# The layer norm behind a causal attention: centring matrix products removed, chunks in pairs, a copy on ScalarE

## The reference, cut to what matters

```
# block B, per head of 8 features, 16 heads; target is _layernorm(x), also the residual
attn = softmax(scores masked to the causal half)
out  = attn @ v
proj = out @ w_proj + b_proj
y    = proj + target
mu, var = mean(y), var(y)
x    = x + (y - mu) * rsqrt(var + 1e-5) * ln_gamma + ln_beta     # called LN M here
# block C
xn   = (x - mean(x)) / sqrt(var(x) + 1e-5)                       # LN C
x    = x + 0.5 * ffn(xn)
```

## The kernel before

| phase | TensorE | VectorE | ScalarE |
|---|---|---|---|
| 0 | `pe_shares` L1449: spreads the inverse denominators | for c = 3 first `dve_invert` L1459; `dve_divide` L1463 | |
| 1 | `pe_project` L1455 | `dve_add` L1467: bias and residual | |
| 2 | LN M centre | copy | square |
| 3 | LN M variance | reciprocal | root |
| 4 | LN M spread | affine, two instructions | |
| 5 | LN C centre | copy | square |
| 6 | LN C variance | reciprocal | root |
| 7 | LN C spread, c < 2 | norm, c < 2 | |

## Time and profile before

### The profile page before, as it was taken

One profiled execution on the slowest core, in us unless ns is written; L12 is line 12 of the kernel. 1 busy time (PEld: TensorE's weight loads), 2 busy tenths in 40 slices (PEclk: granted clock), 3 DMA queues, 4 the chain that ended last, 5 costly groups with the idle time before them and its releaser, 6 DMA issues. The chain is left out here.

```text
span 1345.5 us, 30396 instructions
## 1 busy us (share of the span) xinstructions
PE 1280.2 (95%) x11965; PEld 469.6 (35%) x12028; DVE 1161.1 (86%) x1536; ACT 1056.3 (79%) x2060; POOL 184.0 (14%) x463
## 2 busy tenths in 40 slices
PE   7887999999999998999899999999999999999998
PEld 4343333332333352555322222222222222223454
DVE  6876899999999276765999999999999999998365
ACT  4656788997999826534599999999999999999742
POOL 9234221211111200111100000000000000000100
PEclk9998999999999999899999999999999999999999
DMA  5252210400000003000422000000000000000000
GB/s 133 53 137 42 51 18 14 66 5 12 4 4 4 8 21 79 1 0 30 130 53 53 4 4 12 4 3 4 13 4 3 3 4 13 4 3 3 12 8 24
DMA packets 38526, 35.12 MB, mean 26 GB/s; under 512 B 16080, under 2 KB 31920, under 8 KB 38384
## 3 DMA queue, kind: packets, MB, share of 16 engines
q1 hardware_dynamic: 38384, 33.17, 10.6%
HBM read 17.03 MB, written 9.70 MB: 20 GB/s over the span
## 5 line engine op out<-in xcount | busy, mean ns | idle before, releaser
L1531 DVE TENSOR_REDUCE m_blockmax<-ps 128x2 f32<-128x1024 f32 (+1 forms) x768 | 879.3, 1206 | 26.7 <-PE ps L1352 12.9
L1504 ACT ACTIVATE m_prob<-ps 128x512 f32<-128x512 f32 (+3 forms) x1664 | 845.5, 576 | 46.5 <-PE ps L1390 33.1
L1352 PE MATMUL ps<-m_k_all,m_q_all 64*128 64x512 bf16 (+2 forms) x1732 | 320.0, 374 | 19.6 <-DVE m_blockmax L1531 16.0
L1390 PE MATMUL ps<-m_q_max,m_k_all 64*128 64x512 bf16 (+3 forms) x1664 | 337.3, 366 | 0.5
L1413 PE MATMUL ps<-m_prob,m_v_op 128*9 128x256 f32 x4096 | 317.0, 381 | 0.1
L1352 PEld LDWEIGHTS ps<-m_k_all,m_q_all 64*128 64x128 bf16 x1732 | 81.7, 92 | 347.8 <-DVE m_blockmax L1531 182.0
L1409 PE MATMUL ps<-m_prob,m_v_op 128*9 128x256 f32 (+3 forms) x2560 | 178.1, 351 | 6.2 <-ACT m_pv L1478 5.4
L1390 PEld LDWEIGHTS ps<-m_q_max,m_k_all 64*128 64x128 bf16 x1664 | 143.6, 94 | 91.8 <-ACT m_prob L1504 45.7
L1555 POOL CAST m_maxparts<-m_negmax 128x8 bf16<-128x8 f32 x64 | 14.1, 221 | 712.6 <-DVE m_negmax L1539 707.2
L1413 PEld LDWEIGHTS ps<-m_prob,m_v_op 128*9 128x9 f32 x4096 | 60.9, 88 | 132.2 <-issue 119.0
L803 ACT ACTIVATE m_prob<-ps 128x512 f32<-128x512 f32 x40 | 23.9, 597 | 67.3 <-PE ps L667 55.5
(11 more groups left out here) (226 smaller groups left out, 1043.5 us busy)
## 6 DMA issues: line engine op xcount, KB each, us to landing
m_part<-m_xn SPq DMA_DIRECT2D x48, 128.0 KB, 2.3
ba_parts<-m_part SPq DMA_DIRECT2D x8, 384.0 KB, 3.9
ea_parts<-m_part SPq DMA_DIRECT2D x8, 384.0 KB, 2.6
m_k_all<-ea_parts SPq DMA_DIRECT2D x84, 32.0 KB
m_q_all<-ea_parts SPq DMA_DIRECT2D x84, 32.0 KB
m_k_all<-ba_parts SPq DMA_DIRECT2D x36, 64.0 KB
m_q_all<-ba_parts SPq DMA_DIRECT2D x36, 64.0 KB
ba_sums<-m_pv SPq DMA_DIRECT2D x128, 9.0 KB
```

Of the source, the lines that this page charges most:

```text
L1352: mm = pe.matmul(ps[:, MX + 2 * (u % 2) + j, 0:width], q_all[head, pair, q0:q0 + TW], k_all[head, pair, CW * kc:CW * kc + width], start=Tr ...
L1390: pe.matmul(ps[:, e % ST, q0:CW], k_all[head, pair, TW * i:TW * i + TW], q_max[m % 2][head, q0:CW], start=True, stop=True).then_inc(self.s ...
L1504: nc.scalar.activation(prob[:, (2 * t + j) % NP, q0:CW], ps[:, e % ST, q0:CW], ACT.Exp, scale=SCALE)\
L1531: nc.vector.tensor_reduce(blockmax[:, m % plan.AHEAD, qt, :, kc], ps[:, MX + 2 * (u % 2):MX + 2 * (u % 2) + 2, 0:width], AX.X, ALU.max)\
```

## The change

1. The projection's weights are centred once, on chip (`dve_fold`, behind VectorE's part of the attention loop): the sum of each row of `wproj0`, over 128, is subtracted. The bias is centred by one product of a single column with `centre_of`, behind `pe_loop`. The residual is the output of LN B, so it has mean zero already. With that the projection's sum has mean zero without a centring product: LN M loses its phase 2, four products, four squares from PSUM and four copies. ScalarE now squares `xn` itself (`act_square_of`), and `dve_affine` reads `xn` instead of `cen`.
2. In LN C the copy from PSUM to `cen` goes from VectorE to ScalarE (`act_centre`), behind the square; the spreads wait for it.
3. The order is by pairs: in turn t, chunk c is in phase t - c // 2, seven phases, eight turns.
4. VectorE's reciprocal of chunk 3's denominators moves from the turn of chunk 3's division to phase 1 of chunk 1, between the additions of chunks 0 and 1.
5. The wait for the last copy of the sums moves out of `pe_loop`: in block B it stands ahead of chunk 3's shares, in block F ahead of `pe_shares` of the last chunk.

```diff
+    def dve_fold(self, dve, column):
+        nc, k = self.nc, self.k
+        dve.wait_ge(self.late_in, self.LATE_IN)
+        nc.vector.tensor_reduce(k["fold"][:, 0:1], k["wproj0"][:, :], AX.X, ALU.add).then_inc(self.folded, 1)
+        dve.wait_ge(self.folded, 1)
+        nc.vector.tensor_scalar(k["fold"][:, 1:2], k["fold"][:, 0:1], 1.0 / P, None, ALU.mult).then_inc(self.folded, 1)
+        dve.wait_ge(self.folded, 2)
+        nc.vector.tensor_scalar(k["wproj0"][:, :], k["wproj0"][:, :], k["fold"][:, 1:2], None, ALU.subtract)\
+            .then_inc(self.folded, 1)
+        dve.wait_ge(self.bias_mm, 1)
+        nc.vector.tensor_copy(k["bproj0"][:, 0:1], column).then_inc(self.folded, 1)
...
-        self.nc.vector.scalar_tensor_tensor(out=cen, in0=cen, scalar=self.k["gamma"][:, 0:1], in1=self.ps[:, bank, :],
+        self.nc.vector.scalar_tensor_tensor(out=cen, in0=chunk(src, c), scalar=self.k["gamma"][:, 0:1], in1=self.ps[:, bank, :],
...
+    def act_square_of(self, act, c, src):
+        self.nc.scalar.activation(chunk(self.k["sq"], c), chunk(src, c), ACT.Square).then_inc(self.squared, 1)
+
+    def act_centre(self, act, i, c, bank):
+        act.wait_ge(self.centre_ready, NC * i + c + 1)
+        self.nc.scalar.activation(chunk(self.k["cen"], c), self.ps[:, bank, :], ACT.Copy).then_inc(self.centred, 1)
...
@@ Experts.pe, block F
         else:
+            pe.wait_ge(before.sums_ready, before.plan.count)
             before.pe_shares(pe, last, self.BC)
...
@@ Attention.pe_loop
         pe.wait_ge(self.mx_used, len(plan.steps))
-        pe.wait_ge(self.sums_ready, plan.count)
...
@@ macaron, TensorE
                 att_b.pe_loop(pe)
+                pe.matmul(ps[:, 2 * NC - 1, 0:1], k["centre_of"][:, :], k["bproj0"][:, 0:1], start=True, stop=True)\
+                    .then_inc(constants.bias_mm, 1)
                 def b_end(phase, c):
                     if phase == 0:
+                        if c == NC - 1:
+                            pe.wait_ge(att_b.sums_ready, att_b.plan.count)
                         att_b.pe_shares(pe, c, c)
                     elif phase == 1:
+                        pe.wait_ge(constants.folded, Constants.BIAS_FOLDED)
                         att_b.pe_project(pe, c, NC + c)
                     elif phase == 2:
-                        pe.wait_ge(att_done, c + 1)
-                        norm_m.pe_centre(pe, LN_M, c, xn, c)
+                        norm_m.pe_var(pe, LN_M, c, c, True)
                     elif phase == 3:
-                        norm_m.pe_var(pe, LN_M, c, NC + c, True)
+                        norm_m.pe_spread(pe, LN_M, c, NC + c)
...
-                for t in range(8 + NC - 1):
+                for t in range(8):
                     for c in range(NC):
-                        if 0 <= t - c < 8:
-                            b_end(t - c, c)
+                        if 0 <= t - c // 2 < 7:
+                            b_end(t - c // 2, c)
...
@@ macaron, VectorE
                 att_b.dve_loop(dve)
+                constants.dve_fold(dve, ps[:, 2 * NC - 1, 0:1])
                 def b_end(phase, c):
                     if phase == 0:
-                        if c == NC - 1:
-                            att_b.dve_invert(dve, c)
                         att_b.dve_divide(dve, c, c)
                     elif phase == 1:
+                        if c == 1:
+                            att_b.dve_invert(dve, NC - 1)
+                        dve.wait_ge(constants.folded, Constants.BIAS_FOLDED)
                         att_b.dve_add(dve, c, NC + c)
...
@@ macaron, ScalarE
                 def b_end(phase, c):
-                    if phase == 2:
-                        norm_m.act_square(act, LN_M, c, c)
-                    elif phase == 3:
-                        norm_m.act_root(act, LN_M, c, NC + c)
+                    if phase == 1:
+                        act.wait_ge(att_done, c + 1)
+                        norm_m.act_square_of(act, c, xn)
+                    elif phase == 2:
+                        norm_m.act_root(act, LN_M, c, c)
+                    elif phase == 4:
+                        norm.act_square(act, LN_C, c, c)
+                        norm.act_centre(act, LN_C, c, c)
                     elif phase == 5:
-                        norm.act_square(act, LN_C, c, c)
-                    elif phase == 6:
                         norm.act_root(act, LN_C, c, NC + c)
```

More of the change, by code:

```diff
@@ L103, in __init__ @@
         k["eps"] = n.sb("eps", [P, 1], fp32)
+        k["fold"] = n.sb("fold", [P, 2], fp32)
         k["sign"] = n.sb("sign", [P, 1], fp32)
@@ L126, in __init__ @@
         self.e_split = n.sem("e_split")
+        self.folded, self.bias_mm = n.sem("folded"), n.sem("bias_mm")
     CENTRE_MADE, ROWS_MADE, IDENT_MADE, CLEARED = 2, 2, 3, 6
@@ L246, with __init__ @@
 class Norm:
-    def __init__(self, nc, n, ps, k):
+    def __init__(self, nc, n, ps, k, centres=True):
         self.nc, self.ps, self.k = nc, ps, k
         self.std = k["std"]
-        self.centre_ready, self.centred, self.squared = n.sem("centre_ready"), n.sem("centred"), n.sem("squared")
+        if centres:
+            self.centre_ready, self.centred = n.sem("centre_ready"), n.sem("centred")
+        self.squared = n.sem("squared")
         self.var_ready, self.std_ready, self.inverted = n.sem("var_ready"), n.sem("std_ready"), n.sem("inverted")
@@ L295, in dve_norm, with dve_affine @@
             .then_inc(self.out, 1)
-    def dve_affine(self, dve, i, c, add_to, bank, done):
+    def dve_affine(self, dve, i, c, src, add_to, bank, done):
         dve.wait_ge(self.spread, NC * i + c + 1)
         cen = chunk(self.k["cen"], c)
-        self.nc.vector.scalar_tensor_tensor(out=cen, in0=cen, scalar=self.k["gamma"][:, 0:1], in1=self.ps[:, bank, :],
+        self.nc.vector.scalar_tensor_tensor(out=cen, in0=chunk(src, c), scalar=self.k["gamma"][:, 0:1], in1=self.ps[:, bank, :],
                                             op0=ALU.mult, op1=ALU.mult).then_inc(self.out, 1)
@@ L392, in pe @@
                 for c in (2, 3):
+                    pe.wait_ge(self.norm.centred, NC * self.ln + c + 1)
                     self.norm.pe_spread(pe, self.ln, c, c)
@@ L1888, in _ @@
                 att_b.dve_loop(dve)
+                constants.dve_fold(dve, ps[:, 2 * NC - 1, 0:1])
                 def b_end(phase, c):
                     if phase == 0:
-                        if c == NC - 1:
-                            att_b.dve_invert(dve, c)
                         att_b.dve_divide(dve, c, c)
                     elif phase == 1:
+                        if c == 1:
+                            att_b.dve_invert(dve, NC - 1)
+                        dve.wait_ge(constants.folded, Constants.BIAS_FOLDED)
                         att_b.dve_add(dve, c, NC + c)
                     elif phase == 2:
-                        norm_m.dve_centre(dve, LN_M, c, c)
+                        norm_m.dve_invert(dve, LN_M, c)
                     elif phase == 3:
-                        norm_m.dve_invert(dve, LN_M, c)
-                    elif phase == 4:
-                        norm_m.dve_affine(dve, LN_M, c, x, c, x_done)
+                        norm_m.dve_affine(dve, LN_M, c, xn, x, NC + c, x_done)
                     elif phase == 5:
-                        norm.dve_centre(dve, LN_C, c, c)
-                    elif phase == 6:
                         norm.dve_invert(dve, LN_C, c)
-                    elif c < 2:
+                    elif phase == 6 and c < 2:
                         norm.dve_norm(dve, LN_C, c, xn, c)
-                for t in range(8 + NC - 1):
+                for t in range(8):
                     for c in range(NC):
-                        if 0 <= t - c < 8:
-                            b_end(t - c, c)
+                        if 0 <= t - c // 2 < 7:
+                            b_end(t - c // 2, c)
                 ffn_c.dve_total(dve, 0)
```

7 lines of the change are left out of this document (4 added, 3 removed).

## The result

| | before | changed |
|---|---|---|
| median of the executions timed for this comparison (22 each) | 1352.11 us | 1342.66 us |
| lowest, highest | 1338.41, 1365.73 | 1336.22, 1349.93 |
| the profiled execution, its span | 1347.26, 1345.5 | 1343.33, 1341.6 |

The ratio is 0.9951, 95% interval 0.9929 to 0.9974: 6.6 us less (3.5 to 9.6). It leaves out executions more than 1.5% above the fastest of their kernel (two of the 22 of before); the two medians of the table lie 9.45 us apart, at the upper end of that interval. I had forecast -6.5 us. But I had named a time, 1336.1, from a median of 1342.61 for before, and the changed kernel took 1342.66, outside my range of 1331.5 to 1341.0. The difference fits, as far as an interval of 3.5 to 9.6 us can tell; the level under it was wrong. So two questions stay: whether the stage did what I said, and what sets the level.

A forecast was written before the change was run, and what follows sets the result against it. TensorE's chain of pieces was taken to bound the end of block B, after a late start and a half-clock stretch. Terms -4.9 - 0.8 - 0.7 + 0 - 0.1 = -6.5 us gave 1336.1 from 1342.61; range 1331.5 to 1341.0.

The forecast's parts named there:

- Start of the chain, -4.9 us: End of block B: chunk 3's shares start at 473.25 instead of 478.14 us, as its reciprocal waits only for the load.
- The load: Numerators of chunk 3, block B: taken as 3.4 us, though the skill's fit estimated 2.6, which would be 0.8 us better.
- The chain, -0.8: Chunk 3's shares to first cn_w1 product: the same 21 TensorE pieces, cheaper in pairs, 20.5 us against 21.3.
- the last wait, -0.7: End of the stage: TensorE's 0.7 us wait for the last square goes, since two pieces now lie between.
- rival 2: Block B's end: pairs' round trips exposed or load late, 1 to 4 us come back, 1337 to 1340 us; chance 0.13.
- The clock, 0: Behind TensorE's pause ahead of chunk 3's shares: the 3.4 us half-clock stretch comes back, gaining 0; otherwise 1.7 us.
- Rival 1: Behind the pause in block B's end: clock stays full, -8.2 us, 1334.4 us; chance 0.28.
- rival 5: Chain behind the pause: half clock lasts, 1337.9 us, or slower than before if over 16.4 us long; chance 0.04.
- Block F, -0.1: LN F in block F: variances could start 0.6 us earlier, but only a tenth is gained.
- Rivals 3, 4 and 6: Gain lost behind the stage (1341 to 1344); shorter load (-1.3 us, chance 0.04); reciprocal stays late. First and last together 0.09.

The follow-up runs named there:

- the filled order: Changed kernel, variances of chunks 0 and 1 and projection of chunk 2 moved ahead of chunk 3's shares; ratio to before 0.9881, then 0.9922.
- the filled order with the split wait: The filled order, with chunk 3's reciprocal waiting for the denominators' load alone and its division for the numerators'; ratio to before 0.9925.

## Why the prediction was right about the stage's length and wrong in its time

**The step that failed is the last line of the sum: "Against the median, 1342.61, it gives 1336.1 us".** The median of three executions was taken as the kernel's level, with 2 us for how such medians differ. The 92 executions of before have a median of 1349.0; of medians of three drawn from them only 3% lie at or below 1342.61, and the middle 80% reach from 1345 to 1356. Had I put -6.5 us on 1349.0, it would have been 1342.5. That this comes so near to 1342.66 is partly luck: the 22 executions of this comparison have their median at 1352.11, and from there it would have been 1345.6. The hint was there: the three values shown went from 1341 to 1350, a spread larger than the whole gain, and the profiled execution stood 4.65 us above their median.

What the level hangs on was also in the rows: the half-clock stretches. Added up from windows of 1 us over the whole span, the profile of before has 20.5 us of half clock in 1345.5, that of its repetition 10.3 us in 1339.4. One at about 115 us and one at 1273 or 1279 come in both; the others sit at other places. A second source lies at 113 us: ScalarE waits before a copy of sums for the DMA of an earlier copy, by 5.25 us in before, 2.05 in its repetition, 6.26 in the changed kernel and not at all in the second execution of the filled order (timeline of ScalarE in the four):

```profile
117.13 0.38 ACT L1478 ACTIVATE m_pv<-ps 128x256 f32<-128x256 f32 x1 [5.25 <-DMA ba_sums<-m_pv]
```

```profile
114.20 0.38 ACT L1478 ACTIVATE m_pv<-ps 128x256 f32<-128x256 f32 x1 [2.05 <-DMA ba_sums<-m_pv]
```

```profile
118.61 0.38 ACT L1505 ACTIVATE m_pv<-ps 128x256 f32<-128x256 f32 x1 [6.26 <-DMA ba_sums<-m_pv]
```

```profile
114.11 0.38 ACT L1505 ACTIVATE m_pv<-ps 128x256 f32<-128x256 f32 x1
```

That both together make the whole spread isn't shown; around the line through clock and time a standard deviation of 2.8 us remains.

**Start of the chain, -4.9 us.** The size was close: 12.81 to 8.06 is 4.75. Its reason was half wrong. I gave it to the reciprocal's new place, and called the reordering of TensorE without gain of its own beyond it. The reciprocal alone gives 2.2 us, the pairs alone bring the shares of chunk 3 to 8.0, and with the pairs the reciprocal's place doesn't matter. Both engines stood late, VectorE by its nine instructions and TensorE by its nine pieces; whichever stays in the old order holds the other.

A balance of TensorE's time says where the 6.7 us come from: the stage at full clock less TensorE's waits of over 0.1 us in it, by the timelines.

| | stage, us | waits | work | pieces |
|---|---|---|---|---|
| before | 34.9 | 4.3 | 30.7 | 30 |
| pairs | 31.8 | 3.0 | 28.8 | 30 |
| changed, single chunks | 29.8 | 2.3 | 27.5 | 26 |
| changed | 28.2 | 2.7 | 25.5 | 26 |

The one-column product is not counted as a piece. Of the 6.7 us, 5.2 are work that TensorE no longer has: four centring products, and pieces that are cheaper in pairs. Only 1.5 are waits. TensorE has 26 pieces instead of 30, which is most of it; my sum booked them as "4 pieces fewer ahead" that gain nothing of their own. In single chunks the shares of chunk 3 come 3.4 us later than in pairs, and the stage is only 1.6 us longer; so how early they start is not by itself what the change is worth.

**The load.** 3.4 us, as in the trace of before, and 3.3 to 4.0 over the runs. The fit in the Trainium skill, "DMA: Bandwidth & Descriptors", section "Anatomy of one DMA", gave an estimate of 2.6 us for the 256 KB; none of these executions showed that. The measurement decides.

**The chain, -0.8, and the last wait, -0.7.** 498.00 - 476.18 = 21.82, less 1.7 for the half clock, is 20.1 for 21 pieces; I had 20.5, between bounds of 19.9 and 21.0. So the chain gave 1.2 us and not 0.8. The wait for the last square is gone. Round trips cost nothing in the changed kernel: rival 2 fell.

**The clock, 0.** It came back in the profiled execution, with the same 3.4 us. But that was luck as much as reasoning: of the seven profiles with a pause of over 2 us ahead of these shares four had 3.4 us of half clock in the stage, two 6.8, one none; and the filled order with the split wait had 3.4 us of it, from 488.9 on, with no pause at all. Rival 1 gave a full clock 0.28, but took the fall for a property of the pause, and the runs show that it comes and goes with the same pause; rival 5's lasting half clock didn't come in this stage.

**Block F, -0.1.** 5.39 to 5.27 us.

Rivals 3, 4 and 6: nothing was given back behind (843.6 us in both), the load was not shorter, and the change does what it says.

## What to carry to other kernels

A reload that lies unused for 5 us points to two queues, not one: the engine that makes the operand and the engine that uses it each have their own order, and the point moves only when both reach it early. What the stage gains is then another sum, the work of the engine that bounds it plus its waits. With two instructions behind one load wait, a wait of its own for the smaller load moved more (2.0 us) than reordering around it (0.7 to 0.8). Half-clock time may be corrected by half only where no wait for another engine would have stood in its place; look at the operand's time first. Where single executions spread by more than the gain sought, forecast a difference, take the level with the spread of executions, and look at what sets it before putting a range on it.

## What the runs showed of the hardware that I had not expected

The same program with the same 2.13 us pause of TensorE ran on at full clock in one execution and had 3.4 us at 1.2 GHz in the other. Stretches at half clock lasted 3.4 us or 6.8 in nearly all cases, and 13.7 once, and over 92 executions of before each 0.01 of mean granted clock went with 15.8 us, more than the 13.5 that half speed alone would cost if TensorE were always the bound; in 34 of the changed kernel it was 14.4. Half clock also came behind no pause at all (at 488.88 in the filled order with the split wait), and there it cost next to nothing, because VectorE's affine instructions (0.74 to 0.75 us) and ScalarE's square (0.63 us) ran as long as at full clock and TensorE would have waited for them.
